# A graph network kernel in which the nodes without outgoing edges run one recurrent step ahead

## The reference

```python
def step(h, _):
    messages = h[col] @ W_msg.T + b_msg
    agg = jax.ops.segment_sum(messages, row, num_segments=num_nodes)
    gi = agg @ W_ih.T + b_ih
    gh = h @ W_hh.T + b_hh
    r = sigmoid(i_r + h_r)
    z = sigmoid(i_z + h_z)
    n = tanh(i_n + r * h_n)
    return (1.0 - z) * n + z * h, None
h, _ = jax.lax.scan(step, x, None, length=5)
return x2 + h
```

## Time and profile before

| | us |
|---|---|
| median of 3 runs | 6580.73 |
| lowest, highest | 6575.34, 6590.59 |
| profiled execution, its time | 6588.5 |
| profiled execution, its span | 6586.7 |
| granted TensorE clock, mean share of full | 0.809 |
| busy PE / DVE / ACT / POOL | 4067.0 / 3927.8 / 2455.1 / 3591.8 |
| apply1, first to last scatter | 2524.2 to 3061.9 |
| first-state stage | 3069 to 3388 |
| first gather of steps 1 to 5 | 3388.4, 3968.1, 4551.2, 5135.5, 5722.3 |

### The profile page before, as it was taken

One profiled execution on the slowest core, in us unless ns is written; L12 is line 12 of the kernel. 1 busy time (PEld: TensorE's weight loads), 2 busy tenths in 40 slices (PEclk: granted clock), 3 DMA queues, 4 the chain that ended last, 5 costly groups with the idle time before them and its releaser, 6 DMA issues. The chain is left out here.

```text
span 6586.7 us, 72416 instructions
## 1 busy us (share of the span) xinstructions
PE 4067.0 (62%) x13552; PEld 2209.8 (34%) x13552; DVE 3927.8 (60%) x8010; ACT 2455.1 (37%) x4774; POOL 3591.8 (55%) x3596
## 2 busy tenths in 40 slices
PE   3664445800344650001678998899899889866687
PEld 1322222300122220001555555555555555433343
DVE  5776664348766324565667667766766676544455
ACT  3663222201222210001777436534643663333332
POOL 3555776776577776775037216513721661277766
PEclk8777667955666875555889999999999999977799
DMA  5552113647211545764766435534543553333333
GB/s 216 217 217 81 46 46 113 229 149 261 92 46 46 178 153 159 203 192 129 277 224 191 139 131 176 171 129 144 189 142 129 167 176 131 121 100 100 102 116 106
DMA packets 567288, 977.28 MB, mean 148 GB/s; under 512 B 97608, under 2 KB 250078, under 8 KB 566924
## 3 DMA queue, kind: packets, MB, share of 16 engines
q1 hardware_dynamic: 452524, 761.44, 34.5%
q0 software_dynamic: 100544, 163.41, 8.8%
q10 hardware_dynamic: 14112, 51.39, 2.0%
HBM read 543.13 MB, written 438.34 MB: 149 GB/s over the span
## 5 line engine op out<-in xcount | busy, mean ns | idle before, releaser
L1456 POOL DMA_INDIRECT r_G<-msg_tab,srow x980 | 1021.9, 1043 | 356.1 <-issue 310.4
L845 PE MATMUL cv_psO<-cv_V,cv_cwi 128*128 128x448 f32 x896 | 473.5, 696 | 958.3 <-DVEq L831 958.3
L1464 POOL COPY agg<-r_zero 128x512 f32<-128x512 f32 x196 | 120.3, 614 | 1095.6 <-PE r_psI L1515 1095.6
L1565 ACT ACTIVATE r_r<-r_psR,brz 128x512 f32<-128x512 f32 x490 | 336.7, 687 | 889.8 <-PE r_psR L1510 544.0
L845 PEld LDWEIGHTS cv_psO<-cv_V,cv_cwi 128*128 128x128 f32 x896 | 218.2, 251 | 1213.6 <-issue 690.1
L1503 PE MATMUL r_psHN<-r_hin,whh 128*128 128x512 f32 x980 | 556.5, 652 | 74.2 <-DMA r_hin<-ht_tab 63.3
L1637 DVE TENSOR_TENSOR r_d<-r_hin,r_n 128x512 f32<-128x512 f32 x490 | 340.5, 695 | 355.3 <-ACT r_n L1574 355.3
L1507 PE MATMUL r_psR<-r_hin,whh 128*128 128x512 f32 x980 | 539.0, 634 | 0.0
L1448 POOL DMA_INDIRECT out_dram<-r_m,r_x x392 | 409.5, 1045 | 186.3 <-issue 119.7
L1507 PE MATMUL r_psZ<-r_hin,whh 128*128 128x512 f32 x980 | 509.7, 602 | 0.0
L1523 PE MATMUL r_psS<-r_sel,r_G 128*128 128x129 f32 x1960 | 324.0, 314 | 299.6 <-DMA r_G<-msg_tab,srow 286.4
(11 more groups left out here) (235 smaller groups left out, 8752.6 us busy)
## 6 DMA issues: line engine op xcount, KB each, us to landing
r_hin<-ht_tab SPq DMA_DIRECT2D x490, 256.0 KB
ht_tab<-r_hnew SPq DMA_DIRECT2D x392, 256.0 KB, 2.0
msg_tab<-r_m SPq DMA_DIRECT2D x392, 256.0 KB
o_tab<-o_blank SPq DMA_DIRECT2D x98, 512.0 KB, 6.2
st_h<-h_tab SPq DMA_DIRECT2D x98, 512.0 KB, 3.7
st_o<-o_tab SPq DMA_DIRECT2D x98, 512.0 KB, 4.8
i_x<-x_tab SPq DMA_DIRECT2D x49, 528.0 KB, 3.7
r_x<-x_tab SPq DMA_DIRECT2D x98, 264.0 KB, 2.8
```

The lines of the kernel that those rows point to most:

```text
L845: ins = nc.tensor.matmul(psO[:, h, 0:HW], cwi[m][:], V[i % 2][m][:, HW * h:HW * (h + 1)], start=m == 0, stop=m == 3)
L1456: pool.indirect_dma_start(G[par][:, q, :], None, msg_tab[src_m], bass.IndirectOffsetOnAxis(ap=srow[:, TQ * c + q:TQ * c + q + 1], axis=0)) ...
```

## The change

1. **Idle half a step ahead.** The first-state stage applies the recurrence once to the chunks without edges, and stores both their first messages (`msg0_tab`) and their next ones (`msg1_tab`). Its iterations take one chunk of either half. In steps 0 to 3 the chunks without edges then compute their second to fifth application; step 4 has none. There are three message tables, used in turn.
2. **Outputs of the idle half.** In step 3 they are written to `msg2_tab`; SP reads them back (`staged`, three buffers) in that step's second half, and GpSimd scatters them there. The node numbers for the scatters are copied once by GpSimd (`ids`).
3. **PSUM.** For chunks without edges, t and n are made in place in `r_psHN` and z in place in `r_psZ` or `r_psI` by turns.
4. **Unrolled.** The first-state stage and all steps are written out without hardware loops. `r_G` has four buffers, `r_sel` two; tiles follow the gates by two chunks and the adds by three. The clear of `agg` moves from GpSimd to ScalarE.
5. **Row statistics in apply1.** VectorE makes them from the row buffer there and writes 1/root and -mean/root into two columns of the row; `a_r` has four buffers. The first-state stage uses them from `i_x`.
6. Every stage ends with `retire()`; the early SBUF buffers are given back ahead of the first-state stage.

The core of the diff, SP and VectorE of the first-state stage, and the parts of the steps that the text speaks of:

```diff
+                for i in range(HALF + 3):
+                    if i < HALF:
+                        if i >= 2:
+                            sp.wait_ge(s_relu, 2 * TPC * (i - 1))
+                            sp.wait_ge(s_id, i - 1)
+                        sp.dma_start(xb[i % 2][:], x2h[i]).then_inc(s_xin[i % 2], 16)
+                    if 2 <= i < HALF + 2:
+                        j = i - 2
+                        sp.wait_ge(s_hT, 2 * (j + 1))
+                        sp.dma_start(htv[HALF + j], hT[j % 2][:, 1]).then_inc(s_hst[j % 2], 16)
+                        sp.wait_ge(s_me, 2 * (j + 1))
+                        sp.dma_start(msgh[j], mb[j % 2][:].rearrange("p h t f -> p h (t f)")
+                                     ).then_inc(s_mst[j % 2], 16)
+                    if i >= 3:
+                        j = i - 3
+                        sp.wait_ge(s_h, j + 1)
+                        sp.dma_start(htv[j], hnew[j % 2][:]).then_inc(s_nst[j % 2], 16)
+                        sp.wait_ge(s_me1, j + 1)
+                        sp.dma_start(msgv[1][j], mb1[j % 2][:].rearrange("p t f -> p (t f)")
+                                     ).then_inc(s_m1st[j % 2], 16)
...
+                for i in range(1, HALF + 3):
+                    if i <= HALF:
+                        messages(i - 1)
+                    if 2 <= i < HALF + 2:
+                        update(i - 2)
+                    if i <= HALF:
+                        hidden(i - 1)
+                    if i >= 3:
+                        next_messages(i - 3)
...
+                for i in range(HALF + 1):
+                    if i < HALF:
+                        rows(i)
+                    if i:
+                        states(i - 1)
+                        gates(i - 1)
...
+                for i in range(HALF + 2):
+                    if i < HALF:
+                        transposes(i)
+                    if 1 <= i <= HALF:
+                        messages(i - 1)
+                        gates(i - 1)
+                    if i >= 2:
+                        next_messages(i - 2)
```

```diff
+        JOBS = [(s, h, i) for s in range(STEPS) for h in range(2) for i in range(HALF) if h or s < STEPS - 1]
...
+                            nc.scalar.activation(z[:], z[:], ACT.Sigmoid, bias=brz[:, 1:2]).then_inc(s_z, 1)
+                            act.wait_ge(s_t1, k + 1)
+                            nc.scalar.activation(psHN[k % 2][:], psHN[k % 2][:], ACT.Tanh, bias=bih[:, 2:3]
+                                                 ).then_inc(s_n, 1)
...
+                    n, z = (ns[k % 2], zs[k % 2]) if JOBS[k][1] else (psHN[k % 2], gate_bank(k))
...
+                    if s == FIN0:
+                        for i in range(HALF):
+                            pool.wait_ge(s_sg[i % 3], 16 * (i // 3 + 1))
+                            for t in range(TPC):
+                                pool.indirect_dma_start(out, bass.IndirectOffsetOnAxis(ap=ids[:, 0, i, t:t + 1], axis=0),
+                                                        stg[i % 3][:, t, :], None, bounds_check=N - 1, oob_is_err=False
+                                                        ).then_inc(s_put[i % 3], 16)
```

More of the change, by code:

```diff
@@ L35 @@
 AR = 3
+RR = 4
 SW = P + 1
@@ L1323, in chunk, with transposes @@
[L1323 removed]
+                def transposes(i):
                     for h in range(2):
                         pe.wait_ge(s_relu, TPC * (2 * i + h + 1))
[L1326 removed]
+                        if i:
+                            pe.wait_ge(s_hT, 2 * i + h - 1)
                         for t in range(TPC):
[L1328 to L1331 removed]
@@ L1353, in build @@
+        s_put = [stage_sem(f"r_put{i}") for i in range(3)]
+        s_fin = [stage_sem("r_fin0"), stage_sem("r_fin1")]
         c6 = ExitStack()
@@ L1541, in _, with finish @@
-                steps(pe, step)
+                def finish(k):
+                    pe.wait_ge(s_h, k + 1)
+                    if k:
+                        pe.wait_ge(s_me, k)
+                    for t in range(TPC):
+                        if last(k):
+                            ins = nc.tensor.transpose(psM[:, t, :], hnew[k % 2][:, P * t:P * (t + 1)], ident[:])
+                        else:
+                            ins = nc.tensor.matmul(psM[:, t, :], hnew[k % 2][:, P * t:P * (t + 1)], wmsg[:],
+                                                   start=True, stop=True)
+                    ins.then_inc(s_pm, 1)
```

980 lines of the change are left out of this document (553 added, 427 removed).

## The result

| | us |
|---|---|
| kernel before, median of 4 runs (lowest, highest) | 6585.66 (6575.34, 6613.36) |
| changed kernel, median of 4 runs (lowest, highest) | 6757.67 (6742.46, 6761.71) |
| ratio, 95% interval | 1.025 (1.0214 to 1.0286) |
| changed kernel, profiled execution: time, span, granted clock | 6755.41, 6753.5, 0.791 |

A forecast was written before the change was run, and what follows sets the result against it. Steps, half the program, were bound by GpSimd's gathers, then TensorE. Terms -25 + 21 + 542 - 90 - 1 - 316 + 5 = +136 gave 6724.5 us profiled, 6717 us as median; range 6590 to 6820.

The forecast's parts named there:

- part 4: New stage ahead of the steps: a ring of waiting engines with the x load exposed, 17.2 us an iteration; +542 us.
- The clock's share: New stage: TensorE's matmuls after idling take 2.1 us more per iteration, part of them at the lower clock level.
- part 3: Last step: first half holds gathers only, 258 us less; second half 5.6 us a chunk, 56 less; in all -316 us.
- part 5: apply1 with statistics and four row buffers: -25 us; semaphore clearings: +21 ahead of the new stage, +5 at the end.
- part 1: Idle-half updates in steps 0 to 3: PSUM operands stop VectorE stretching GpSimd's gathers, 246 us for 196; 90 us less.
- The next limit is VectorE's own work for a chunk: Idle half: after the gathers' 4.99 us a chunk, VectorE's work limits next, 4.82 us between two r_d operations.
- the term of -90: Steps 0 to 3: shorter gathers save 19 us in step 0 and 23.6 in each of the other three.
- part 2: Ends of halves: 2.4 us a step gained, later last stores and step 3's scatters cost time; sum -1 us.
- stretching: apply1: bn_stats, all in SBUF, may stretch GpSimd's scatters; not shown, 25 us at 0.5 us a chunk; -25 taken, not -30.
- The 72.6 us of waits: apply1: GpSimd's waits for VectorE within the scatters' 538.6 us, taken away by four row buffers instead of two.
- three clearings: Stage changes before apply1's scatters: semaphore clearing costs 5.2 us each.
- Rival C: Long straight code of four engines stalls, 2.1 us every 8 of 441 chunks: +116, 6833 us; chance 0.08.

The follow-up runs named there:

- the run with TensorE kept busy: Changed kernel plus nine further matmuls of 512 columns behind the gates in each iteration of the new stage, results unread: 6698.93 us.
- the early load: Changed kernel with SP issuing the new stage's load of x for iteration i+1 ahead of iteration i's stores: 6554.56 us, ratio 0.9947.

## Why the prediction was right, and where not

- **The new stage (part 4)**: right in mechanism, and the size is partly luck. An iteration was forecast at 17.2 us and is 17.2, but two terms in it were off by 0.7 us each and cancelled. In the iteration shown, the load is issued 12.8 us behind the first Relu (13.5 forecast) and the Relus start 4.4 us behind that (3.7 forecast; why the load takes longer isn't shown). Without the exposed load 13.1 was forecast and 13.3 measured. The clock's share was taken as 2.1 us for both. Against the run with TensorE kept busy, in which the message matmuls end 6.7 us behind the first Relu, it is 1.6 us in the changed kernel (8.3) and 2.4 with the early load (9.1).
- **The last step (part 3)**: -316 forecast, -311 with the 5 us that part 5 puts at the end, and -316.3 measured. 48 intervals of r_psI take 6457.8 to 6725.6, 5.6 us each.
- **PSUM operands (part 1)**: the mechanism was right: gathers beside SBUF operations take up to 1.47 us in the kernel before, and with PSUM operands none takes over 0.96 in steps 1 to 3. The Trainium skill ("SBUF — State Buffer", Who interferes with whom), weighed there, infers that such an operation leaves descriptor writing alone. The lengths of these gathers do not bear that out. The Trainium skill's rule, in the same section, for GpSimd operations that read SBUF may still be what shows here, since a gather takes its row numbers from srow in SBUF, and no run tells the two apart. But the step "The next limit is VectorE's own work for a chunk", with 4.82 us, failed. The next limit was a ring through three engines at 5.26 us. 49 x 5.26 + 10 = 268 us is what the half takes, whatever the gathers do, so the term of -90 is -55.6 in the trace, and the operands themselves gave none of it. The gathers did shorten as forecast, by 83 us over the four steps; 27 us came back as a longer way from the last gather to r_psI. The two r_d of the earlier trace rows were 4.82 apart because the one before had been late; a steady interval has to be read over several chunks, and the shortest steady one of before is 5.06.
- **Ends of the halves (part 2)**: no gain of 2.4 us a step is to be seen; the way from the last gather to r_psI grew from 13 to 20 us, since the gathers end early. At the ends of steps the way from the last r_psI to the next gather grew by 1.3, 0.9 and 1.0 us (1.5 forecast) and ahead of step 4 by 3.9 (4.5). With no delay and the messages stored at a step's end it is 10.1 us instead of 12.4.
- **apply1 (part 5)**: the net is right (-10.4, -9 forecast), from two terms that were off and cancelled. From the first scatter's start to the last one's end it takes 511.5 us, where 499 and 5 for stretching were taken. The 72.6 us of waits that were read as part of the 538.6 held 24.0 us from ahead of the first scatter, and the wait of 11 us near the end stayed, as 11.9. The stretching did not come: beside bn_stats, all in SBUF, scatters take at most 978 ns (median 969). The first scatter was 16.8 us later, where 15.6 for three clearings and 9 for the statistics were expected, but this proves little: in the twelve further profiles, with the same code ahead of it, the first scatter starts anywhere between 2524.5 and 2543.5 us.
- **Rival C**: no stalls of that kind. Its argument against, that unrolled GpSimd code shows no others, was misread. The second halves stand at 290.1 us for 48 intervals, before and after. Hitches of the kind of the earlier trace rows stood six times between the gathers of steps 0 to 3 of the kernel before, 2.1 to 2.8 us each; in the changed kernel the longest gap between two gathers of a step is 0.93 us.

Where the gain of the last step went is the question of this case, and the answer is that 542 us of a longer stage stood against it, of which 462 were order, not work.

## What to carry to other kernels

Draw the ring of a loop's waits before costing its engines: a loop in which every engine waits for the one before runs at the sum of their latencies, and there a load one place earlier, a dependent part one iteration later or one add ahead of its neighbour is worth more than faster operations. Before an operation is made cheaper, find what would be last in its place over several steady iterations, not from one pair of rows. When work is moved to where data is ready sooner, its queue positions come along, and they decided the sign here.

## What the runs showed of the hardware

- Nine idle-time matmuls of 512 columns in each iteration raised the granted clock of the stage from 0.71 to 1.00 and took 1.2 us off an iteration of 17.2. A better order gave a clock of 1.00 with no extra work (TensorE busy for 311 of 358 us).
- A gather of 0.94 us beside a VectorE tensor_tensor on SBUF alone took 0.94 to 1.47 us, by where the two overlapped; where VectorE's operations of the update had a PSUM operand, the 784 gathers of steps 0 to 3 took 0.94 to 1.01. Indirect scatters beside bn_stats on SBUF kept their 0.97 us.
- Hitches of 1.8 to 3.3 us on GpSimd between gathers ("issue") appear in all four kernels with two gather buffers and in none of the ten with four. Why isn't shown.
